# Two joined pairs of states per group in a scan kernel: an accumulating DMA from GpSimd adds one weighed state to the next, TensorE sums them as one

## The reference

```
c  = rotate(x, delta_t)                      # amplitudes and angles per sequence
xn = layernorm(c)
for d in (forward, reversed):                # two directions
    u     = silu(conv4(xn @ W_in))           # 256 channels
    dt, B, C = split(u @ W_x)                # 64, 16, 16
    delta = softplus(dt @ W_dt + b)
    for n in 16 states:                      # the scan, over the 128 tokens
        h_n[t] = exp(delta[t]*A_n) * h_n[t-1] + delta[t]*u[t]*B_n[t]
    y_d = (sum over n of h_n * C_n + u*D) * silu(z)
x1 = x + glu(gelu([y_f, y_r] @ W)) + c
x2 = expert_ffn(x1)                          # the merged weights of one of 8 experts per sequence
out = x1 + ffn(x2)                           # gate, up, h1, h2, w3
```

## Time and profile before

| what | us |
|---|---|
| median of 3 runs | 1061.58 (1057.41 to 1061.61) |
| the profiled execution, its own time | 1059.2 |
| its span in the profile | 1057.0 |
| busy: PE, DVE, POOL, ACT | 944.2, 920.4, 855.6, 779.4 |

### The profile page before, as it was taken

The page is one execution under the profiler, slowest core; times in us unless marked ns, Lnnn a source line. Parts: engine busy times, 40 slices in busy tenths (PEclk is TensorE's granted clock), DMA queues, the critical chain, the costliest instruction groups (busy, mean ns, idle before and its releaser), DMA issues.

```text
span 1057.0 us, 13719 instructions
## 1 busy us (share of the span) xinstructions
PE 944.2 (89%) x4320; PEld 603.2 (57%) x4320; DVE 920.4 (87%) x722; ACT 779.4 (74%) x1241; POOL 855.6 (81%) x428
## 2 busy tenths in 40 slices
PE   4698688879989999999999999989889987998897
PEld 3455456656645566555755575546655575556556
DVE  1988999999999999999999999898999999978701
ACT  4858767878598868987788869886687867777522
POOL 0777999989987998989897999899788898866400
PEclk9797699889999999999999999999999998999999
DMA  3855655673556645755456464664646564555100
GB/s 114 285 177 198 203 164 165 178 210 103 181 166 189 190 130 150 239 146 169 164 178 202 117 190 154 194 178 130 158 134 184 159 187 130 142 172 150 39 1 16
DMA packets 97670, 167.43 MB, mean 158 GB/s; under 512 B 9920, under 2 KB 33408, under 8 KB 97344
## 3 DMA queue, kind: packets, MB, share of 16 engines
q1 hardware_dynamic: 97600, 166.57, 52.6%
HBM read 159.19 MB, written 7.34 MB: 158 GB/s over the span
## 4 chain that ended last, share of the span: by engine, by line
PE 44%; ACT 17%; issue 16%; DVE 14%; POOL 8%; DMA 1%; SPq 0%; DVEq 0%; POOLq 0%; ACTq 0%
DVE bank_d L980 9%; PE bank_y L1274 9%; PE bank_m L1104 8%; PE bank_m L1180 7%; POOL state L595 5%; PE bank_m L1187 5%; ACT bank_d L745 4%; ACT L626 4%; PE bank_m L1153 3%; DVE state L978 2%; POOL state L600 2%; PE bank_m L1194 2%; PE bank_m L1162 2%; PE bank_m L1169 2%; PE bank_m L1122 1%
## 5 line engine op out<-in xcount | busy, mean ns | idle before, releaser
L595 POOL TENSOR_TENSOR state<-du,b_rows 128x1024 f32<-128x1024 f32 (+1 forms) x288 | 629.1, 2210 | 53.6 <-PE bank_y L1274 46.1
L980 DVE TENSOR_TENSOR_SCAN bank_d<-bank_d,state 128x1024 f32<-128x1024 f32 (+1 forms) x225 | 461.2, 2050 | 32.0 <-ACT bank_d L745 30.9
L745 ACT ACTIVATE bank_d<-delta,a_neg 128x512 f32<-128x512 f32 (+1 forms) x540 | 322.6, 634 | 78.2 <-DVE state L985 73.5
L1274 PEld LDWEIGHTS bank_y<-ident,state 128*128 128x128 f32 x2048 | 243.9, 147 | 92.5 <-issue 63.4
L1274 PE MATMUL bank_y<-ident,state 128*128 128x128 f32 x2048 | 270.2, 284 | 25.9 <-DVE gated L996 12.5
L985 DVE TENSOR_TENSOR state<-bank_d,c_rows 128x1024 f32<-128x1024 f32 (+1 forms) x225 | 248.8, 1106 | 7.7
L600 POOL TENSOR_TENSOR state<-state,c_rows 128x1024 f32<-128x1024 f32 (+1 forms) x63 | 134.1, 2128 | 16.7 <-DVE state L978 15.7
L1104 PE MATMUL bank_m<-xnT,w_conv 128*128 128x508 f32 (+7 forms) x288 | 118.4, 557 | 4.5 <-DVE x1T L1005 2.4
L1187 PE MATMUL bank_m<-hidA,h_s 128*128 128x512 f32 (+1 forms) x256 | 112.5, 585 | 5.7 <-ACT hidA L817 4.6
L1180 PE MATMUL bank_m<-hidB,h_s 128*128 128x512 f32 (+1 forms) x256 | 107.8, 573 | 0.8 <-DVE hidB L1019 0.8
L978 DVE TENSOR_TENSOR_SCAN state<-bank_d,state 128x1024 f32<-128x1024 f32 (+1 forms) x45 | 92.0, 2044 | 3.4 <-ACT bank_d L745 3.4
(11 more groups left out here) (152 smaller groups left out, 1047.6 us busy)
## 6 DMA issues: line engine op xcount, KB each, us to landing
b_rows<-bc_store SPq DMA_DIRECT2D x256, 256.0 KB, 5.0
c_rows<-bc_store SPq DMA_DIRECT2D x256, 256.0 KB, 4.7
wsel<-merged SPq DMA_DIRECT2D x32, 512.0 KB, 3.5
merged<-hidA SPq DMA_DIRECT2D x8, 512.0 KB, 3.1
h_s<-in_h SPq DMA_DIRECT2D x2, 1024.0 KB, 9.2
xin<-in_x SPq DMA_DIRECT2D x7, 256.0 KB, 5.1
out<-cT SPq DMA_DIRECT2D x7, 256.0 KB, 5.3
wsel<-in_factors SPq DMA_DIRECT2D x8, 160.0 KB, 3.5
```

Of the source, the lines that this page charges most:

```text
L595: nc.gpsimd.tensor_tensor(split(unit_state(u)), du[:, d, :, :width(g)], per_half(b_rows, u), ALU.mult).then_inc(S.bx_ready, 1)
L745: ins = act.activation(split(unit_decay(u))[:, h], delta[:, d, h, :width(g)], ACT.Exp, scale=a_neg[:, h, n:n + 1])
L980: dve.tensor_tensor_scan(decay, decay, drive, 0.0, ALU.mult, ALU.add).then_inc(S.scanned, 1)
L1274: ins = pe.matmul(bank_y[:, h, s * P:(s + 1) * P], split(unit_state(u))[:, h, s * LEN:(s + 1) * LEN], ident[:, :], start=(n == 0 and s == ...
```

## The change

- **Joined pairs.** In each group units 12 and 26 are `JOINED`. After GpSimd has come one unit past such a unit u, it issues a DMA that adds the state of unit u-1 into the state of unit u, inside SBUF (`join`; 512 KB of each in a wide group, 256 KB in a narrow one). TensorE no longer sums u-1; it waits on the semaphore `joined` and sums u two units later than it would have (`JOIN_LAG = 2`), so at u+4. The first matmul of that sum counts as the release of u-1's slot, the last as that of u's.
- GpSimd weighs units 20 and 25 in place of 21 and 26 (`POOL_UNITS`); the number stays seven.
- `RING` is 9 in place of 8, paid for by `ROWS = 4` in place of 6; `ROW_LEAD` is 5 in place of 6, so rows of B are asked for one unit later.
- `shift` of the norm is one GpSimd multiplication after the power, no longer two or four activations on ScalarE.
- Many numbers of the tables move by 0.5 to 1 unit, a few by more.

The code of it (of the tables only two lines):

```diff
-RING = 8
-ROWS, C_ROWS = 6, 4
+RING = 9
+ROWS, C_ROWS = 4, 4
-POOL_UNITS = (3, 8, 12, 17, 21, 26, 30)
+POOL_UNITS = (3, 8, 12, 17, 20, 25, 30)
+JOINED, JOIN_LAG = (12, 26), 2
-GPS = {"power": -32.5, "residual": -11.5, "delta": (-4.0, 5.0), "inputs": (-3.5, 8.0)}
+GPS = {"power": -33.0, "residual": -10.5, "delta": (-4.0, 5.5), "inputs": (-3.5, 7.0)}
-ROW_LEAD, C_LEAD = 6, 3
+ROW_LEAD, C_LEAD = 5, 3
...
+        def joined(u):
+            return u % UNITS in JOINED
+
+        def summed_at(u):
+
+            if joined(u + 1):
+                return summed_at(u + 1)
+            return u + SUM_LAG + (JOIN_LAG if joined(u) else 0)
+
+        summed_as = {u: i + 1 for i, u in enumerate(sorted(range(TOTAL), key=lambda u: (max(summed_at(u), u - u % NST + HELD + SUM_LAG), joined(u) or joined(u + 1), u)))}
...
                 nc.gpsimd.tensor_tensor(rstd[:, :n], var_eps[:, :n], half_power[:, :n], ALU.pow).then_inc(S.rstd_ready, 1)
+                pool.wait_ge(S.rstd_ready, g + 1)
+                nc.gpsimd.tensor_tensor(shift[:, :n], neg_mean[:, :n], rstd[:, :n], ALU.mult).then_inc(S.shift_ready, 1)
...
-                wait(pool, S.states_summed, u + 1 - RING)
+                wait(pool, S.states_summed, summed_as.get(u - RING, 0))
...
+            def join(u):
+
+                wait_product(pool, u - 1)
+                wait_product(pool, u)
+                nc.gpsimd.dma_start(unit_state(u), unit_state(u - 1), accum_op=ALU.add).then_inc(S.joined, 16)
...
+                if u is not None and joined(u):
+                    join(u)
...
             def normalise(g):
-                act.wait_ge(S.rstd_ready, g + 1)
-                for t in range(sequences(g)):
-                    ins = act.activation(shift[:, t:t + 1], neg_mean[:, t:t + 1], ACT.Copy, scale=rstd[:, t:t + 1])
-                ins.then_inc(S.shift_ready, 1)
                 act.wait_ge(S.shift_ready, g + 1)
...
             def sum_states(u):
                 g, d, n = unit(u)
-                wait_product(pe, u)
+                if joined(u):
+                    pe.wait_ge(S.joined, 16 * sum(joined(v) for v in range(u + 1)))
+                else:
+                    wait_product(pe, u)
...
+                        if joined(u) and h + s == 0:
+
+                            ins.then_inc(S.states_summed, 1)
...
-                    for v in range(u - HELD if u % NST == HELD else u, u + 1):
-                        sum_states(v)
+                    for v in range(u - HELD if u % NST == HELD else u, u + 1):
+                        if summed_at(v) <= at:
+                            sum_states(v)
+                u = unit_at(at, -SUM_LAG - JOIN_LAG)
+                if u is not None and joined(u) and u % NST >= HELD:
+                    sum_states(u)
```

More of the change, by code:

```diff
@@ L72 @@
        "w3": 74.0}
-GPS = {"power": -32.5, "residual": -11.5, "delta": (-4.0, 5.0), "inputs": (-3.5, 8.0)}
+GPS = {"power": -33.0, "residual": -10.5, "delta": (-4.0, 5.5), "inputs": (-3.5, 7.0)}
 BX_LEAD, WEIGH_LAG = 3, 1
 SUM_LAG, HELD = 2, 3
-TURN = (19.0, 36.0)
-LOADS = {"x": -40.0, "bc_store": (-7.5, -1.0), "selected": (23.5, 26.5, 28.5, 31.0), "store": 76.0, "back": 3.0}
-ROW_LEAD, C_LEAD = 6, 3
-FIRST_GROUP = {"ur1": 5.5, "h1_1": -2.0, "h2_0": 0.0, "power": -3.5, "bc_store": 1.0, "ur0": 10.0, "z0": 6.5, "z1": 8.5,
[5 rows of a table removed]
-               "w3": 0.5, "gate1": -1.0, "delta": -1, "inputs": 0, "normalise": -1.0, "gated": 0.5, "back": 2,
[3 rows of a table removed]
@@ L96 @@
-LAST_GROUP = {"up0": 2.5, "uf1": 5.5, "h2_2": 9.5, "delta": -1, "ur0": 1.0, "h2_0": 18.0, "h2_1": 21.0, "h2_3": 10.0,
[4 rows of a table removed]
+TURN = (19.0, 35.0)
+LOADS = {"x": -41.5, "bc_store": (-7.5, 1.0), "selected": (24.5, 28.0, 29.0, 29.0), "store": 76.0, "back": 3.0}
+ROW_LEAD, C_LEAD = 5, 3
+FIRST_GROUP = {"ur1": 3.5, "h1_1": -1.5, "h2_0": 0.0, "power": -3.5, "bc_store": 1.0, "ur0": 9.0, "z0": 6.5, "z1": 8.5,
[5 rows of a table added]
+               "w3": 1.0, "gate1": -2.5, "delta": -1, "inputs": 2, "normalise": -1.0, "gated": 0.5, "back": 1.5,
[3 rows of a table added]
@@ L101 @@
+LAST_GROUP = {"up0": 2.5, "uf1": 5.5, "h2_2": 8.5, "delta": -1, "ur0": 5.0, "h2_0": 16.0, "h2_1": 19.5, "h2_3": 9.0,
[4 rows of a table added]
               "scale": 0.5, "glu1": -1.0, "store": 5.5, "norm": 0, "back": 2.5, "selected:2": 5.0, "gated:1": -1.5,
[1 row of a table removed]
[1 row of a table added]
               "copied:1": -0.5, "selected:3": -3, "sigmoid": -3.0, "gelu:0": 5.5, "delta:0": 0.0, "dt01": -1.5,
               "bc_store:1": -2.5, "inputs:0": -0.5, "silu": -1.5, "inputs:1": -0.5, "copied:0": 0.5, "residual": 6,
[1 row of a table removed]
-SECOND_GROUP = {"scale": 4.0, "rotate": 2.5, "power": 3.0, "residual": -3.0, "back": 3, "store": 4, "z0": 4.5, "hid3": 2,
[5 rows of a table removed]
[2 rows of a table added]
@@ L113 @@
+SECOND_GROUP = {"scale": 4.0, "rotate": 2.5, "power": 3.0, "residual": 1.0, "back": 3, "store": 4, "z0": 4.5, "hid3": 2,
[5 rows of a table added]
                 "h2_0": 0.5, "h2_3": 0.5, "hid2": 0.5, "wo": -0.5, "copied:0": -1, "up1": 0.5, "ur0": 0.5, "ur1": 0.5,
[1 row of a table removed]
-NEXT_TO_LAST = {"res": 0.0, "residual": -2.5, "copied": 0.5, "h2_1": 4.5, "glu0": 0.0, "hid1": 1.5, "ur1": -1.0, "store": -5,
[1 row of a table added]
+NEXT_TO_LAST = {"res": 0.0, "residual": -10.5, "copied": 0.5, "h2_1": 4.5, "glu0": 0.0, "hid1": 1.5, "ur1": 2.5, "store": -5,
                 "sigmoid": 1, "h1_2": -1.5, "normalise": 1.5, "h1_0": 0.5, "h1_1": -2.0, "dbc1": 0.0, "x": 1, "selected": 1.5,
[6 rows of a table removed]
[6 rows of a table added]
+                "softplus": 0.5}
@@ L277, in build @@
             abs_ready exp_ready log_ready delta_ready du_ready starts_marked
-            stored_bc0 stored_bc1 b_loaded0 b_loaded1 b_loaded2 b_loaded3 b_loaded4 b_loaded5 c_loaded0 c_loaded1 c_loaded2 c_loaded3
-            exp_done bx_ready scanned unit_done weighed states_summed
+            stored_bc0 stored_bc1 b_loaded0 b_loaded1 b_loaded2 b_loaded3 c_loaded0 c_loaded1 c_loaded2 c_loaded3
+            exp_done bx_ready scanned unit_done weighed joined states_summed
             gated_ready y_copied y_turned glu_log glu_ready wsel_loaded stored""".split()
@@ L283, in build @@
         stored_bc = (S.stored_bc0, S.stored_bc1)
-        b_loaded = (S.b_loaded0, S.b_loaded1, S.b_loaded2, S.b_loaded3, S.b_loaded4, S.b_loaded5)
+        b_loaded = (S.b_loaded0, S.b_loaded1, S.b_loaded2, S.b_loaded3)
         c_loaded = (S.c_loaded0, S.c_loaded1, S.c_loaded2, S.c_loaded3)
```

19 lines of the change are left out of this document (10 added, 9 removed), and 57 rows, old and new, of tables (FILL, FIRST_GROUP, LAST_GROUP, NEXT_TO_LAST).

## The result

The changed kernel takes **1073.78 us** (median of four runs, 1069.85 to 1074.41); the kernel before took 1060.96 us beside it. The ratio is **1.012** with a 95% interval of 1.0086 to 1.0153: slower by 12.8 us. The forecast was 1053, the range ended at 1067. The profiled execution took 1073.53 us with a span of 1071.3 us.

What follows compares the result with a forecast made beforehand. VectorE's own work was taken as a near floor, TensorE counting only where the chain runs through it; -6.0 - 1.6 + 2.0 - 2.0 = -7.6 from 1059.2 gave 1051.6, 1054.0 by the median, predicted 1053; range 1041 to 1067.

Steps and rivals of the forecast that it cites:

- C (late): Joins land 12 us after issue or later, TensorE stands still in its block of sums: 1072 us, chance 0.16.
- E (issue held off): Each GpSimd DMA issue waits for the running VectorE instruction, up to 2.29 us: +4, so 1056 us, chance 0.05.
- VectorE's own work, which the change leaves as it is, sets a floor: VectorE is busy 96% of groups 1 to 7, leaving 35.5 us; its unchanged work was taken as a near floor.
- Rival B: VectorE's floor takes what TensorE gives; only ScalarE's -1.6 and GpSimd's +2.0 remain: 1060 to 1062 us, chance 0.26.
- Rival B's second way, the clock: An emptier TensorE may have more stretches at 1.2 GHz; eight more would eat 14 us.
- Sums left out, -6.0: 128 of 2048 TensorE matmuls go, relieving it of 14.0 us; 43% counted: -6.0 us, bounds 0 and -14.0.
- 43% share of the chain: Of 223 us of TensorE's sums of states, 95 us lie on the chain that ended last: 43%.
- `shift` moved, -1.6: ScalarE loses 32 activations, 6.8 us; 23% counted: -1.6 us, bounds 0 and -6.8.
- Rows of B, 0: Four rows, one unit less lead: landing takes 5.0 us within 7.0 us, so hidden: 0.
- bound of +2: Other bound for the rows of B: +2 us if joins hold up these transfers.
- The ring, 0: Nine slots give `drive` one unit more; unit 20's scan keeps 2.5 us of slack: 0.
- The moved times, -2.0: A quarter of 8.1 us more VectorE idleness from 681 to 806 us than in group 3: -2.0 us, bounds 0 and -8.1.

Runs made afterwards that it cites:

- e2: The changed kernel with the tables' old numbers, units 21 and 26, and `shift` on ScalarE; joins, nine slots and four rows of B stay: 1078.0 us, ratio 1.0188.
- e16: The kernel before with GpSimd weighing units 20 and 25 in place of 21 and 26, and `shift` made on GpSimd: 1072.81 us, ratio 1.0102.
- e9: The changed kernel with the ring back at eight slots and rows of B back at six, joins kept: 1073.25 us, ratio 1.0116.
- e10: The changed kernel without joins, with the ring at eight slots and six rows of B: 1075.62 us, ratio 1.0122.
- e14: The kernel before with GpSimd weighing units 20 and 25 in place of 21 and 26, plus both joins (12 and 26): 1069.63 us, ratio 1.0085.
- e5: The kernel before with GpSimd weighing units 20 and 25 in place of 21 and 26, nothing else: 1056.81 us, ratio 0.997.
- e13: The kernel before with GpSimd weighing units 20 and 25 in place of 21 and 26, plus the join into 12 alone: 1069.57 us, ratio 1.0089.
- e18: The changed kernel with `shift` put back on ScalarE, all else as changed: 1071.4 us, ratio 1.0116.
- e6: The kernel before with four rows of B in place of six and their lead 5 in place of 6, ring of eight: 1064.39 us, ratio 1.0044.
- e7: The kernel before without early scans, units 8 and 17 scanned from a bank like the others: 1075.81 us, ratio 1.0148.
- e8: The changed kernel without early scans, units 8 and 17 scanned from a bank like the others: 1079.4 us, ratio 1.0175.
- e4: The changed kernel with only GpSimd's times of `delta` and `du` put back to 5.0 and 8.0: 1072.99 us, ratio 1.0124.

## Why the prediction was wrong

**The mechanics of the join were right.** One issue holds GpSimd for 0.88 us (1.0 taken). The 512 KB land after 8.5 us (7 taken); TensorE waited 2.3 us for it, where I expected under 2 (with the old times and nine slots, in e2, it waited 15.6). Rivals C (late) and E (issue held off) did not occur, and the scan of unit 20 did not come to wait for its `drive` in the changed kernel. The Trainium skill's page "DMA: Bandwidth & Descriptors" (section on the anatomy of a DMA from GpSimd) gives an estimate of 3.2 us by its fit, which has no addition in it; the measurement, 8.5, decides, and it is 2.7 times that.

**The step that failed first** is "VectorE's own work, which the change leaves as it is, sets a floor". The instructions are the same, their time is not: an early scan of a wide group takes from 2.3 us to 5.4 in the changed kernel and to 7.6 in e16, by what GpSimd has started, and 6.8 us came to VectorE in this way. Rival B rests on the same sentence, and no rival had a loss from there. The row was on the page (2678 ns for `early`, 2044 ns for the same scan from a bank), and I had read past it because it is no large group. Rival B's second way, the clock, did come in part: TensorE spent 21 us more at the lower level, 11 of them busy, and that took 5.5 us of its relief.

**Sums left out, -6.0.** This is the largest term that failed. The size of the relief was nearly right (11.1 us busy of 14.0 in this group), though only 2.5 us of it are left in TensorE's total. Its 43% share of the chain was not: in the changed layout the joins give nothing that can be measured (e9 beside e10, 1.0116 and 1.0122), and in the old one they cost 12 us by themselves (e14 against e5, 1.0085 and 0.997). The rows of e13 point to the slots that a pair holds, those of e2 to waits for the landing; which it is stays open. What the chain shows is who was last at each point, not what comes back when one of them is shortened.

**`shift` moved, -1.6.** On the kernel before it cost 1.3%, 14 us (e16 beside e5), the larger part of them only with early scans, and in the changed kernel it is worth nothing that can be measured (e18).

**Rows of B, 0.** +0.44% alone (e6). The bound of +2 was too low: 7.0 us of room for a landing of 5.0 left nothing for an issue that comes late; where it comes late wasn't looked into.

**The ring, 0.** The scan of unit 20 did not wait, as forecast, but `drive`'s wait for TensorE was to fall from 46.1 us and is 48.1.

**The moved times, -2.0.** Group 6, the stretch from 681 us before, did get shorter, as assumed and by more: from its first scan to that of group 7 it took 124.0 us and takes 120.1. Its granted clock rose from 0.96 to 0.99, so this need not be the moved numbers' doing. (It begins 16 us later in the changed kernel, so the two rows at 681 us, with VectorE at 113.6 and 118.8 us, are not quite the same work.) Against this, groups 1 to 5 and 7 grew. The clock is at its lowest beside before's in groups 1 and 7, with tables of their own for the second and next to last group; which numbers of them matter wasn't tried. With joins and the new rooms, the new times, units and `shift` together bring 1.0188 (e2) to 1.012; without joins and rooms they cost 1.2% (e10), where -3.6 us were forecast for `shift` and times. They are fitted to the new layout and don't make up for it.

**What stays open.** The loss is 12.8 us, and its parts don't add up to it: `shift`, units and times alone bring all of it, the joins alone bring it nearly, and together they bring it once. About 9 us are a gain from early scans that the changed kernel no longer has (e7, e8), 3.6 are the change without them. How the 9 split between the scans' own length (6.8 us in the profiled execution), the waits behind them and the lower clock isn't settled: e4 and e18 have 3 to 5 us less of early scans, and at most 2.4 us less of time, which is inside their scatter, and by the comparison at one clock about half of the 12.8 us goes with it. That collisions cost time is shown for `shift` on the kernel before (e5, e16); that they are the main part of the changed kernel's loss is argued, not shown.

## What to carry to other kernels

Before pricing edits by an engine's share of the chain, look for one operation that has two durations in the profile (here a scan with a mean of 2.04 and of 2.68 us): it marks a contest whose outcome an edit may change, also one that only touches another engine (here nine small multiplications). Compare the granted clock too, stretch by stretch, before a difference is put down to instructions. A buffer that is held longer to save work of an engine must be priced as a buffer: who asks for it next, and who waits for that one. Where edits don't add up, try each alone on the old kernel and take what holds; here that is the swap of the units alone (0.997), the one version that was not slower than before.
